# A transformer block in float32 on one core: the upper query tiles' probabilities transposed by VectorE and placed by DMA instead of by TensorE

## The reference, cut to what matters

```
xn = layernorm(x)
q, k, v = split(xn @ qkv_w + qkv_b)                 # per head: 1024 x 128 each
scores  = q @ k.T + slope[h] * (j - i), j <= i      # causal, slope[h] = 2 ** (-h / 2)
ctx     = softmax(scores) @ v
attn    = ctx @ out_w + out_b
W       = lut[idx]                                  # three weights, from a table of 16 values
ffn     = (silu(xn @ Wg.T) * (xn @ Wu.T)) @ Wd.T
out     = x + attn + ffn
```

## Time and profile before

| | |
|---|---|
| median of three runs | 531.49 us |
| the profiled execution: its time, its span | 532.76 us, 530.9 us |
| TensorE busy in matmuls | 515.0 us, 97% of the span |
| VectorE | 410.5 us, 77% |
| GpSimd | 340.6 us, 64% |
| ScalarE | 303.8 us, 57% |
| DMA engines, mean share | 7.4% |

### The profile page before, as it was taken

The page is one execution under the profiler, slowest core; times in us unless marked ns, Lnnn a source line. Parts: engine busy times, 40 slices in busy tenths (PEclk is TensorE's granted clock), DMA queues, the critical chain, the costliest instruction groups (busy, mean ns, idle before and its releaser), DMA issues.

```text
span 530.9 us, 10648 instructions
## 1 busy us (share of the span) xinstructions
PE 515.0 (97%) x3216; PEld 465.3 (88%) x3216; DVE 410.5 (77%) x1068; ACT 303.8 (57%) x653; POOL 340.6 (64%) x395
## 2 busy tenths in 40 slices
PE   7898999999999999999999999999999999989998
PEld 7687889998999889988998899988998899878897
DVE  6798787888778887878788877897897869764451
ACT  3566665657564846666565656474666556654330
POOL 3475977578676856686757866795658657872400
PEclk8999999999999999999999999999999999999999
DMA  7300100001000100010001000010000000000001
GB/s 269 111 21 1 40 22 21 2 20 41 0 20 20 40 0 20 0 40 20 20 0 38 21 0 20 20 40 0 20 0 0 20 1 2 1 1 1 1 21 59
DMA packets 7429, 13.14 MB, mean 25 GB/s; under 512 B 1008, under 2 KB 3184, under 8 KB 7280
## 3 DMA queue, kind: packets, MB, share of 16 engines
q1 hardware_dynamic: 7408, 12.88, 7.4%
HBM read 11.83 MB, written 1.05 MB: 24 GB/s over the span
## 4 chain that ended last, share of the span: by engine, by line
POOL 41%; issue 34%; PE 18%; DVE 4%; ACT 1%; POOLq 1%; DMA 1%; DVEq 0%; ACTq 0%
POOL w_ffn L1028 16%; POOL work L1003 15%; POOL pad L1002 3%; POOL qk_w_lo L983 3%; PE ps_s L393 2%; PE ps_s L394 2%; PE ps_s L395 2%; PE ps_u L393 2%; PE ps_u L395 2%; PE ps_u L394 2%; POOL o_w_lo L1017 2%; POOL v_w_lo L988 1%; PE ps_t L512 1%; PE ps_t L395 1%; PE ps_t L394 1%
## 5 line engine op out<-in xcount | busy, mean ns | idle before, releaser
L1028 POOL TENSOR_TENSOR w_ffn<-w_ffn,term 128x1088 f32<-128x1088 f32 x60 | 152.6, 2543 | 0.0
L659 ACT ACTIVATE work<-work,neg_max 128x128 f32<-128x128 f32 (+7 forms) x128 | 98.7, 771 | 35.0 <-DVE neg_max L846 34.9
L666 ACT ACTIVATE p_t_hi<-ps_t 128x512 fp32r<-128x512 f32 (+1 forms) x192 | 86.2, 484 | 37.0 <-PE ps_t L512 35.5
L879 DVE TENSOR_TENSOR p_t_lo<-ps_t,p_t_hi 128x512 fp32r<-128x512 f32 (+1 forms) x192 | 98.9, 542 | 7.9 <-ACT p_t_hi L666 7.8
L1003 POOL TENSOR_SCALAR work<-work,inv_sum 128x128 f32<-128x128 f32 (+7 forms) x128 | 102.2, 799 | 0.0
L846 DVE CUSTOM_DVE_ANT_0 work<-ps_s,alibi 128x128 f32<-128x128 f32 (+7 forms) x128 | 96.1, 751 | 4.1 <-issue 4.1
L1002 POOL TENSOR_TENSOR pad<-entry 128x1 f32<-128x1 f32 x128 | 26.7, 208 | 102.8 <-DVE inv_sum L873 102.3
L512 PE MATMUL ps_t<-ident,work 128*128 128x128 f32 x576 | 84.6, 273 | 7.2 <-DVE p_t_lo L879 6.1
L512 PEld LDWEIGHTS ps_t<-ident,work 128*128 128x128 f32 x576 | 68.5, 140 | 15.5 <-DVE p_t_lo L879 3.9
L393 PE MATMUL ps_u<-p_t_hi,v_hi 128*128 128x512 f32 x192 | 69.5, 362 | 0.0
L393 PE MATMUL ps_s<-qk_hi 128*128 128x256 f32 (+2 forms) x192 | 67.3, 350 | 1.4 <-DVE neg_max L846 1.4
(11 more groups left out here) (125 smaller groups left out, 1171.6 us busy)
## 6 DMA issues: line engine op xcount, KB each, us to landing
qk_raw<-w_qk SPq DMA_DIRECT2D x16, 256.0 KB, 2.6
w_ffn<-idx SPq DMA_DIRECT2D x1, 2176.0 KB, 11.4
v_raw<-w_v SPq DMA_DIRECT2D x8, 256.0 KB, 2.6
o_raw<-w_o SPq DMA_DIRECT2D x8, 256.0 KB, 2.5
out<-acc SPq DMA_DIRECT2D x8, 128.0 KB, 1.7
acc<-x SPq DMA_DIRECT2D x2, 256.0 KB, 2.9
acc<-x SPq DMA_DIRECT2D x1, 512.0 KB, 5.1
term<-b_out SPq DMA_DIRECT2D x1, 128.0 KB, 6.3
```

The source lines that it names most:

```text
L659: act.activation(slot(i), slot(i), ACT.Exp, bias=neg_max[:, col:col + 1], scale=-1.0, accum_out=row_sum[:, col:col + 1]).then_inc(exp_done, 1)
L666: act.activation(p_rows(0, i, g), ps_t[:, room, 0:len(turned(i, g)) * P].rearrange("p (j q) -> p j q", q=P), ACT.Copy).then_inc(p_hi, 1)
L879: dve.tensor_tensor(p_rows(1, i, g), ps_t[:, room, 0:len(turned(i, g)) * P].rearrange("p (j q) -> p j q", q=P), p_rows(0, i, g).bitcast(F3 ...
L1028: pool.tensor_tensor(piece, piece, term[:, :], ALU.add).then_inc(term_added, 1)
```

## The change

For 15 of the 16 heads the upper tiles leave TensorE's transposes. ScalarE scales them (its own `norm`), VectorE transposes them in 32x32 blocks from `work` to a new buffer `blocks` (two instructions a tile, `turn_blocks`), and when the fourth tile is done SyncE issues 16 DMAs, one for each pair of 32-partition groups, that carry the blocks from partitions 32a to partitions 32g of `p_t[1]` (`move`). There ScalarE makes hi of four chunks (`upper_hi_of`, in steps 4 and 5 of the next head) and GpSimd makes lo in place (`upper_lo_of`). TensorE reads the result in runs of 32 columns (`upper_context`), in step 7 of the next head, where before it was step 3, 4 or 5. The last head keeps the transposes by TensorE, in `TAIL`.

Beside it: q keeps one head only (`q_all`), k two; the tiles' units are in another order; the product of the lower tiles of the head p = 0 comes in the next head (`_pv0`); `alibi` is halved in place instead of made from `distance` and `slope`; the look-ups are in steps 1, 3, 5, 7 and their sums in 1, 3, 6, 7; the weights' lo parts are made in other steps; v's weights are loaded and split one pair later; GpSimd clears `blocks` (3712 columns) at the start and no longer writes 16 slopes.

```diff
-QK_W_AT = 4
+QK_W_AT = 6
-TERM_AT = 0
-SUM_AT = 1
+TERM_AT = (1, 3, 5, 7)
+SUM_AT = (1, 3, 6, 7)
+BAND_TIGHT = 3 * B32
+BAND = QT * P + 3 * BAND_TIGHT + P
+MOVES = QUADS * QUADS
+CHUNKS = 4
...
     STEADY: [
-        (("q1", 0), ("_out0", 0), ("k1", 1), ("_out1", 1), ("nq0", 2), ("_pv1-", 3), ("_pv1", 4),
-         ("v0", 5), ("v1", 6), ("nk0", 6), ("pv0", 7), ("v2", 7)),
-        (("k1", 0), ("q1", 0), ("v3", 1), ("_out2", 1), ("_out3", 2), ("_pv1-", 4), ("_pv1", 4),
-         ("nk0", 6), ("nq0", 6), ("pv0", 7)),
+        (("q1", 0), ("k1", 1), ("nk0", 2), ("_out0", 3), ("nq0", 4), ("_out1", 5), ("_pv1-", 7), ("_pv1", 7),
+         ("v0", 7), ("v1", 7)),
+        (("q1", 0), ("k1", 1), ("nk0", 2), ("_pv0", 2), ("v2", 3), ("nq0", 4), ("_out2", 4), ("v3", 5),
+         ("_out3", 6), ("_pv1-", 7), ("_pv1", 7), ("pv0", 7)),
...
+            def move(n, p):
+
+                sp.wait_ge(blocks_turned, n * (2 * QT) + p * QT + QT)
+                if not (isinstance(n, int) and n == 0 and p == 0):
+                    kind = FIRST if isinstance(n, int) and n == 0 else STEADY
+                    sp.wait_ge(unit_done, number(n, kind, p, "_pv1"))
+                for a in range(QUADS):
+                    for g in range(QUADS):
+                        sp.dma_start(p_t[1][g * B32:(g + 1) * B32, PT_UPPER + a * BAND:PT_UPPER + (a + 1) * BAND].bitcast(F32),
+                                     blocks[a * B32:(a + 1) * B32, g * BAND:(g + 1) * BAND]
+                                     ).then_inc(blocks_moved, 16)
...
+            def upper_context(bank, pr, js):
+
+                for j in js:
+                    m = first_tile(j)
+                    at = j * P if j < QT else QT * P + (j - QT) * BAND_TIGHT
+                    bands = [t[:, PT_UPPER:].rearrange("p (a x) -> p a x", x=BAND)[:, :, at + m * B32:at + P]
+                             .rearrange("p a (i c) -> p a i c", c=B32) for t in p_t]
+                    last = three(ps_u[:, bank, :].rearrange("p (i a c) -> p a i c", i=QT, c=B32)[:, :, m:, :],
+                                 both(v, slice(None), j, slice(pr * D, pr * D + D)), bands,
+                                 j == 0, j == NT - 1)
...
+            def norm(n, p, i):
+
+                act.wait_ge(inv_ready, tile_no(n, p, i) + 1)
+                col = p * NT + i
+                act.activation(slot(i), slot(i), ACT.Copy,
+                               scale=inv_sum[:, col:col + 1]).then_inc(upper_normed, 1)
+
+            def upper_hi_of(n, p, chunk):
+
+                act.wait_ge(blocks_moved, n * (32 * MOVES) + (p - 1) * (16 * MOVES) + 16 * MOVES)
+                act.activation(chunk_rows(0, chunk), chunk_rows(1, chunk).bitcast(F32),
+                               ACT.Copy).then_inc(upper_hi, 1)
...
+                        if i == NT - 1:
+                            exp(n, p, i)
+                            norm(n, p, i - 1)
+                            norm(n, p, i)
                         for name, step in units_of(kind, p):
                             if step == i and is_split(name):
                                 hi_of(n, p, name, bank_of(kind, p, name), number(n, kind, p, name))
-                        exp(n, p, i)
+                        if i < NT - 1:
+                            exp(n, p, i)
+                            if i > QT:
+                                norm(n, p, i - 1)
+                        if i in (4, 5) and not (kind == FIRST and p == 0):
+                            for chunk in (0, 1) if i == 4 else (2, 3):
+                                upper_hi_of(n, p, chunk)
...
+            def turn_blocks(n, p, i):
+
+                dve.wait_ge(upper_normed, n * (2 * QT) + p * QT + i - QT + 1)
+                if i == QT and not (isinstance(n, int) and n == 0 and p == 0):
+                    dve.wait_ge(blocks_moved, n * (32 * MOVES) + p * (16 * MOVES))
+                for g, count in enumerate((QT, i - QT + 1)):
+                    at = g * QT * P
+                    to = band_rows(blocks[:, :], i - QT, g, count).rearrange("p a j c -> p j a c")
+                    last = dve.transpose(to, slot(i)[:, at:at + count * P].rearrange("p (j a c) -> p j a c",
+                                                                                     j=count, c=B32))
+                last.then_inc(blocks_turned, 1)
...
+                        if i == QT + 2 and upper:
+                            turn_blocks(n, p, QT)
+                        if i == NT - 1:
+                            if upper:
+                                turn_blocks(n, p, QT + 1)
+                            invert(n, p, i)
+                            if upper:
+                                turn_blocks(n, p, QT + 2)
...
+                            if "_pv1" in name and upper:
+                                turn_blocks(n, p, NT - 1)
...
+            pool.memset(blocks[:, :], 0.0).then_inc(made, 1)
...
+            def upper_lo_of(n, p, chunk):
+
+                pool.wait_ge(upper_hi, n * (2 * CHUNKS) + (p - 1) * CHUNKS + chunk + 1)
+                rows = chunk_rows(1, chunk)
+                pool.tensor_tensor(rows, rows.bitcast(F32), chunk_rows(0, chunk).bitcast(F32),
+                                   ALU.subtract).then_inc(upper_lo, 1)
...
-                        if not (kind == FIRST and p == 0 and i == 0):
+                        if 1 <= i <= QT:
                             norm(n, p, i - 1)
+                        if i in (4, 5) and not (kind == FIRST and p == 0):
+                            for chunk in (0, 1) if i == 4 else (2, 3):
+                                upper_lo_of(n, p, chunk)
```

341 lines of the change are left out of this document (188 added, 153 removed), and 3 rows, old and new, of the table UNITS.

## The result

The changed kernel takes 543.85 us (median of four runs, 542.21 to 551.68), the kernel before, run beside it, 531.41: a ratio of 1.0215, interval 1.0186 to 1.0244. It is slower by 12.4 us, where 516.1 was forecast; the range ended at 543. The profiled execution took 543.26 with a span of 541.5, against 532.8 and 530.9.

The account below looks back on a forecast made before the run. TensorE was taken as full before, a chain over three engines after: 54.4 a pair plus 0.6 of lock, 55.0 from 57.2. Seven pairs save 15.4: 532.8 to 517.4, less 1.3 for the median, 516.1 us; range 497 to 543.

Parts of the forecast that it names:

- Part 1: TensorE loses the upper tiles' transposes, 5.7 us a pair, leaving 51.2; products over runs of 32 columns cost nothing extra.
- Parts 2 to 4: Loads a pair: VectorE stays at 46.8 us, ScalarE rises from 34.9 to 41.3, GpSimd from 40.8 to 48.4.
- the walk: Following the chain at heads' ends and VectorE's steps 0 to 6: 8.2 + 15.8 + 10.1 + 20.3 = 54.4 us a pair.
- the sum by the queues: Combining the engines' loads by a chain, not the largest load: a pair from 57.2 to 55.0 us, lock included.
- The first rival: TensorE stays the bound in steady heads, since waits at the heads' ends close: 488.6 us, chance 0.12.
- GpSimd's lo chunks end 1 to 2 us before the eviction that needs the product: In the head's last step, GpSimd's lo parts of the upper tiles are ready 1 to 2 us early.
- The ends, priced at nothing: GpSimd's clearing at the start and the tail's extra turn and chunks were taken to cost no time.
- 4.5 are free there: TensorE is busy for 66.5 of the last 71.0 us, so the tail's added work costs nothing.
- The lock: VectorE's step-5 look-up waits for GpSimd's subtractions: 0.6 us a pair added; by the skill's rule 1.2 a head, 2.4 a pair.
- The move: SyncE's 16 DMAs a head take 10.5 us, from issues of 0.47 each; bounds 7.5 and 27.
- the prediction's second rival: The move lands late at ScalarE's first chunk in step 4, deciding from 10.5 us in p = 0: 547, chance 0.14.
- near 710: Time in us if the move takes 27 us, its 16 landings one behind the other, adding 16 + 13 a pair.

Follow-up runs that it names:

- pof_spread: As passes_order_first, with ScalarE's four chunks spread over steps 4, 5, 5 and 6 instead of two each in steps 4 and 5: 544.1 us.
- half_lo: The changed kernel with GpSimd subtracting only the first half of each upper-tile chunk's columns, the rest left out: 547.4 us.
- first_unit: The changed kernel with the first head's lower product pv0 in its own step 7, not the second head's step 2: 541.8 us, ratio 1.0175.
- warm_mid_tail: passes_order_first plus seven zero matmuls and the fourth look-up between v0's and v1's lo parts in p = 0 heads, gate_up 0 between tail turns 4 and 5: 537.5 us.
- small_terms: The changed kernel with look-ups and their sums cut to 64 of 1088 columns, the rest left out: 549.4 us.
- first_last: The changed kernel with the edits of first_unit and `last` together: 541.5 us, ratio 1.0168.
- last: The changed kernel with the last head's fourth look-up moved behind the lo parts of its turned tiles 4 and 5: 546.6 us (median; runs 540.4 to 559.4).
- passes_order_first: The changed kernel with pv1's hi passes first for all chunks, pv1 evicted before tile 7's scaling, and first_unit's edit: 544.0 us.

## Why the prediction was wrong

**What held.** Part 1: the transposes are gone, and the runs of 32 columns cost nothing; TensorE reads 53.6 a pair and not 51.2. By the pitches of its matmuls from start to start the work left is 50.9, as priced. Of the rest 1.5 stands behind nine waits, since a matmul behind a wait lasts 0.50 in place of 0.40 and overlaps nothing; the other 1.2 is spread over the pair. Parts 2 to 4: every load within 1.4 us a pair. GpSimd's start cost nothing (the clearing took 3.19 us, 3.6 forecast). No wait for the move is over 0.9 us.

**The step that failed in the steady heads** is the walk in "the sum by the queues". It gave p = 1 (steps 0 to 6 and its end) 20.3 + 8.2 = 28.5, and p = 0 15.8 + 10.1 = 25.9. Measured are 28.5 and 28.5. VectorE's ends of heads came out at 8.8 and 9.8 (mask of tile 7 at 237.43, next head's mask at 246.24; 207.91 and 217.71). The term that was mis-sized is steps 0 to 6 of p = 0: 15.8 forecast, 18.7 measured (189.17 to 207.91). In it are three waits that the walk did not have: 1.37 for the turned tile behind ScalarE's chunks, which I had put into p = 1 alone; 0.95 for q's hi part, behind TensorE's 1.44 for GpSimd's scaling; and 1.07 of lock in one look-up, where 0.6 a pair was taken. They do not add up. The walk went along VectorE and left GpSimd out, and the two are tied by the lock: the look-up of step 5 can't end before GpSimd's first chunk does. `pof_spread` took 0.95 of the 1.37 away, and steps 0 to 6 still took 18.7. Where the look-up starts at the same 14.4 us and meets no lock, in two p = 0 heads of `half_lo`, they took 17.7. So 1.07 is shown to be the lock's, with the 1.37 hidden in front of it; for the other 1.9 the waits of the trace are all there is, and which of them binds stays open.

**The sum also averaged TensorE over the pair.** "51.2 a pair" hides that the change moves pv0 of p = 0, and v2, from the p = 0 head into p = 1: eleven units and nine become nine and eleven. The p = 1 head is then full. Heads are cut here at VectorE's masks; by TensorE's own list, from one head's first score matmul to the next's (215.51 to 242.95), its work is 27.4, without a gap, and the other 1.1 of the 28.5 is left over from p = 0. No experiment brought its mean below 28.5, whichever engine was relieved. The first rival, TensorE as the bound, was right for one head in two. The new table of units, read by head, would have told it; I read it by pair.

**"GpSimd's lo chunks end 1 to 2 us before the eviction that needs the product"** failed. They end at 211.3, TensorE waits 1.9 us for them, pv1 ends at 212.3 and ScalarE, done scaling at 212.38, evicts at 212.44. That these two meet within 0.2 us is why half_lo could not end the head earlier: there too the eviction stands behind the scalings (154.43 to 156.41), and the clock fell besides.

**The ends, priced at nothing,** are the other error, of about the same size. I forecast 15.4 off, and 10.5 came on: 25.9 apart. Of these the six steady pairs are 12.7 (13.2 forecast, 0.5 gained), the first pair 9.2 (2.2 off forecast, 7.0 on), the last pair and tail 5.2, less 1.1 for the earlier start. The words "4.5 are free there" took TensorE's free time for room. The added work came in front of matmuls that were then waited for: TensorE's waits of 0.35, 1.73 and 4.19 in the last head and 0.99 and 4.33 in the first stand against 1.75 and 1.69 as the longest there before. first_unit and warm_mid_tail each gave back part, which shows the mechanism for those parts; the rest of the ends is read from the trace only.

**The lock** is real. Its sum was priced well, its place was not: sixty look-ups take 1.10 us in the mean, up to 2.34, and 1.03 before, so 0.5 a pair more; but 1.07 of it falls on the step-5 look-up of p = 0, with no wait to fill. The row was also read too mildly: "nearly always" 0.84 holds for 42 of the 60 look-ups before, and the subtraction in the earlier trace rows ends 1.09 us after the look-up's start, not 0.8; 0.83 is what the look-up lost by it. In small_terms a look-up of 64 columns takes 2.46 us beside GpSimd's chunks. The Trainium skill (SBUF — State Buffer, SBUF: two separate sides) says that the loser of the port pair fully blocks for the other's whole instruction. The trace agrees, and the 1.2 a head of that rule would have been nearer in p = 0.

**The move.** It takes 10.06 us to issue and 2.3 to land, 12.4, where 10.5 was taken from an issue of 0.47. By the prediction's second rival it "decides from 10.5 us on in p = 0". It did not decide, since the p = 0 head was 2.6 us longer than walked; it is the next thing behind. The 8.7 us that the prediction worked out from the skill's figure for ports did not apply: the pace does not follow the bytes. (That rival's worst case, "near 710", comes to 719 by its own terms.)

**Still open:** what the p = 0 head would be with a shorter move (fewer or parallel issues), and whether pv0 of p = 0 put back into its own head in all pairs, as first_unit does in the first, evens the two heads. Neither was tried.

## What to carry to other kernels

Take the load of each engine by the smallest repeated stage, here a head and not a pair: a full engine in one and a chain in the other average to "nearly full", and what is taken off the engine is worth something in the first alone. Where an engine was full, price the stretches in which the taken work was also the cover, above all the first and the last round. And before you shorten one of several paths that meet, look how far the next one is behind: here GpSimd's lo chunks, ScalarE's scalings and the move lay within some 1.3 us.

## What the runs showed of the hardware

- TensorE's granted clock fell to the lower level, 0.50 of full, behind single waits of 1.8 to 4.3 us, though not behind each (one of 2.05 in first_last and one of 3.57 in `last` left it at 1.00), and behind 1.15 and 0.83 close together in four of six heads of passes_order_first. TensorE then worked at it for 3 to 5 us; 512-column matmuls then start 0.43 us apart, 256-column ones 0.21. The changed kernel's 0.32, 1.17 and 0.42 over five us left it at 1.00. Relieving another engine can so cost time: half_lo gathered the waits into one, and took 547.4. Seven matmuls over zeros in these waits kept the clock at 1.00.
- An issue of a DMA from SBUF to SBUF over 32 partitions takes 0.63 us of SyncE's queue, with 119 KB as with 128 bytes; one of 256 KB from memory over 128 partitions takes 0.33.
- A look-up of VectorE that starts inside a subtraction or sum of GpSimd ends 0.58 us behind the end of that instruction, where it takes 0.84 alone; and GpSimd's 1024-column subtraction takes 2.41 us alone and 2.89 where a look-up gets in between.
- VectorE's block transpose in float32 takes as long as its two-source subtraction of the same width: 0.69 us for 512 columns, 0.68 there.
